# Both scans of a chunk pair back to back on VectorE, its statistics and normalise behind them

## The reference, cut to what matters

```
z = sigmoid(h @ Wz.T + bz);  t = tanh(h @ Wh.T + bh)      # here Wz = Wh, bz = bh
a = clip(1 - z, 1e-8, 1 - 1e-8)
s[i] = a[i] * s[i-1] + z[i] * t[i]                        # along the sequence
h = layernorm(s + h if layer > 0 else s) * gamma + beta
```

## Time and profile before

| | |
|---|---|
| median of 3 runs | 461.15 us (461.13 to 468.23) |
| the profiled execution, its own time | 462.03 us |
| its span, first to last instruction | 460.2 us |
| mean granted TensorE clock | 0.917 |
| busy share of the span: PE, DVE, ACT, POOL | 78%, 70%, 49%, 39% |

### The profile page before, as it was taken

How to read it: one execution, slowest core, us unless ns; L and a number is a source line. 1 busy time by engine, 2 the same in 40 slices (tenths; PEclk the granted TensorE clock), 3 DMA queues, 4 the chain that set the end, 5 groups by cost and what they waited for, 6 DMA issues and landing times.

```text
span 460.2 us, 8251 instructions
## 1 busy us (share of the span) xinstructions
PE 359.6 (78%) x2861; PEld 278.6 (61%) x2861; DVE 323.2 (70%) x917; ACT 227.5 (49%) x402; POOL 179.5 (39%) x278
## 2 busy tenths in 40 slices
PE   1666767676674459886799799999699989997991
PEld 1245636354362246655678668968568868785791
DVE  6988987988977665868527927688928687447416
ACT  2435786988955254336225257434267424623520
POOL 6235563656546306720038400259400268403211
PEclk9997898999977588889599989999989999999998
DMA  5600000000000000000000000000000000000000
GB/s 159 191 0 0 3 1 0 1 0 2 1 0 0 1 1 1 1 0 1 1 1 2 2 1 2 1 0 23 0 0 0 0 0 25 1 3 0 24 0 24
DMA packets 8968, 5.48 MB, mean 12 GB/s; under 512 B 700, under 2 KB 8424, under 8 KB 8936
## 3 DMA queue, kind: packets, MB, share of 16 engines
q1 hardware_dynamic: 8936, 5.07, 3.8%
HBM read 4.02 MB, written 1.05 MB: 11 GB/s over the span
## 4 chain that ended last, share of the span: by engine, by line
PE 52%; DVE 24%; ACT 12%; issue 9%; POOL 1%; DMA 1%; POOLq 0%; DVEq 0%; ACTq 0%
PE bank L761 9%; PE bank L694 5%; PE bank L658 5%; PE bank L502 4%; ACT work L921 3%; PE bank L528 3%; PE bank L746 3%; PE bank L669 2%; PE bank L671 2%; PE bank L540 2%; PE bank L747 2%; PE bank L751 2%; PE bank L542 2%; DVE tmp L285 2%; DVE tmp L288 2%
## 5 line engine op out<-in xcount | busy, mean ns | idle before, releaser
L469 POOL TENSOR_TENSOR h_fwd<-ident_bf,mneg 128x512 bf16<-128x512 bf16 x32 | 33.1, 1041 | 81.8 <-DVE mneg L1251 59.7
L1004 ACT ACTIVATE z_and_t<-bank,vec 128x512 f32<-128x512 f32 x64 | 43.8, 694 | 41.8 <-PE bank L751 41.7
L761 PE MATMUL bank<-w_s,z_and_t 128*128 128x128 f32 x512 | 61.4, 277 | 0.0
L761 PEld LDWEIGHTS bank<-w_s,z_and_t 128*128 128x128 f32 x512 | 59.2, 192 | 3.1 <-ACT z_and_t L1004 2.3
L988 ACT ACTIVATE probs<-bank 128x512 f32<-128x512 f32 x64 | 37.7, 595 | 42.9 <-PE bank L671 42.9
L1255 DVE TENSOR_REDUCE mx<-bank 128x4 f32<-128x512 f32 x64 | 43.6, 686 | 21.2 <-PE bank L658 20.4
L446 POOL TENSOR_TENSOR a_bwd<-a_bwd,a_fwd 128x512 f32<-128x512 f32 x11 | 14.6, 1327 | 102.7 <-DVE a_fwd L1312 102.7
L658 PE MATMUL bank<-k_st,q_m 128*128 128x128 f32 x256 | 48.0, 313 | 8.2 <-DVE mx L1255 7.1
L658 PEld LDWEIGHTS bank<-k_st,q_m 128*128 128x128 f32 x256 | 40.3, 205 | 11.2 <-DVE mx L1255 5.4
L540 PE MATMUL bank<-ident,work 128*128 128x128 f32 x128 | 37.4, 319 | 10.7 <-DVE work L1136 7.9
L502 PE MATMUL bank<-ident,work 128*128 128x128 f32 x144 | 25.5, 306 | 10.8 <-DVE work L296 6.8
(11 more groups left out here) (179 smaller groups left out, 866.8 us busy)
## 6 DMA issues: line engine op xcount, KB each, us to landing
x_rows<-in_x_dram SPq DMA_DIRECT2D x4, 256.0 KB, 3.1
probs<-in_L_ffn_W_dram SPq DMA_DIRECT2D x1, 1024.0 KB, 5.4
w_s<-in_L_ffn_W_dram SPq DMA_DIRECT2D x4, 256.0 KB, 6.3
out_dram<-ctx_rows SPq DMA_DIRECT2D x3, 256.0 KB, 2.2
ctx_rows<-in_ctx_dram SPq DMA_DIRECT2D x1, 256.0 KB, 3.2
out_dram<-ctx_rows SPq DMA_DIRECT2D x2, 128.0 KB, 1.8
fw_rows<-in_L_xcond_fusion_W_dram SPq DMA_DIRECT2D x1, 128.0 KB, 3.9
wq_s<-in_L_ffn_Wq_dram SPq DMA_DIRECT2D x1, 64.0 KB, 3.0
```

The costliest lines, as they stand in the source:

```text
L469: pool.tensor_tensor(diag_of(j), ident_bf[:, :].unsqueeze(1).to_broadcast([P, 4, P]), mneg[:, t % 2, 4 * j:4 * j + 4].unsqueeze(2).to_broa ...
L761: last = pe.matmul(dst[:, t * P:(t + 1) * P], hid[:, e % 2, c, t * P:(t + 1) * P], w2_s[:, e, c, :], start=(c == 0), stop=(c == FC - 1))
L1004: act.activation(hid[:, e % 2, c, :], bank[6 + (c + flip) % 2][:, :], ACT.Relu, bias=col(R_B1 + FC * e + c)).then_inc(s["relu_r"], 1)
```

## The change

Only VectorE's window is reordered. The same instructions run with the same waits; nothing is added or removed. Before, the order is: inflow(2j), stats(2j-2), scan(2j), stats(2j-1), inflow(2j+1), norm(2j-4), scan(2j+1). After it is: inflow(2j), scan(2j), inflow(2j+1), scan(2j+1), stats(2j-2), stats(2j-1), norm(2j-4). It holds for all pairs of all four layers; the two windows behind the last pair (scans=False) keep their order.

```diff
                 if scans:
                     inflow(l, 2 * j, layer0)
                     link()
-                if rows:
-                    stats(l, 2 * j - 2)
                 if scans:
                     scan(l, 2 * j, layer0)
                     link()
-                if rows:
-                    stats(l, 2 * j - 1)
                 if scans and not layer0:
                     inflow(l, 2 * j + 1)
-                before_norm()
-                if normed:
-                    norm(l, 2 * j - 4)
                 if scans:
                     link()
                     scan(l, 2 * j + 1, layer0)
                     link()
+                if rows:
+                    stats(l, 2 * j - 2)
+                    stats(l, 2 * j - 1)
+                before_norm()
+                if normed:
+                    norm(l, 2 * j - 4)
```

## The result

The kernel after takes 499.81 us (median of 4 runs, 498.04 to 502.38) against 461.14 us before: 1.082 times as long, interval 1.077 to 1.087. Its profiled execution took 498.04 us, with a span of 496.2 us (36.0 more than before) and a mean granted clock of 0.885.

What follows compares the result with a forecast made beforehand. It took a loop of waits between TensorE and ScalarE to bound the kernel, and the change to close a loop through VectorE's norm: 5.0 us in layer 0 plus 27.0 over 12 windows of 9.7 us gave 493 us, range 481 to 502.

Steps and rivals of the forecast that it cites:

- clock always low: Case that TensorE's clock is low at the norm in every window: 497 to 501 us, chance 0.18.
- Layer 0: Layer 0: later stats delay layer_norm and decay, so its last norm ends at 50.3 instead of 45.37, 5.0 us.
- The loop through norm: Norm, to_rows, affine, gates, second inflow, scan, stats, norm: 8.90 us per window, 10.22 at the low clock.
- The loop through GpSimd: Stats, layer_norm, next decay, first scan, second inflow: inflow could start at E + 4.1, against E + 4.18 over TensorE.
- The clock: TensorE's transposes take 1.32 us more at the low level, expected in six windows of ten: 9.7 us per window.
- the second rival: Clock low at each norm, the same period repeating the same state: 10.22 us per window, 499 us, chance 0.18.
- One wait removed alone would give nothing back: The ways over GpSimd and TensorE come to the same length, so removing either wait alone gains nothing.
- What follows the windows: Behind the last norm with scans: rows unchanged, about 325 us as before, 2 us either way for the clock.
- only the hole: Rival: norm's place does not matter, only VectorE's unfilled 1.6 us per window: 12.8 us more, 474 us, chance 0.05.
- faster: Rival: the second scan ends sooner and releases the odd to_rows sooner: 447 to 452 us, chance 0.02.
- covered: Rival: VectorE's 0.71 us slack and the time before gate_in absorb it: within 2%, up to 470 us, chance 0.04.
- The clock is low at each norm: Rival: TensorE's pause right ahead of the transposes lowers the clock every window: 38.2 us more, 499 us, chance 0.18.

Runs made afterwards that it cites:

- e3_gates_first: Kernel after, with ScalarE doing gates(2j+1) ahead of affine(2j-6): 489.75 us, ratio 1.060 against the kernel before.
- e4_decay_first: Kernel after, with GpSimd doing the next window's first decay ahead of layer_norm in layers 1 to 3: 494.60 us, ratio 1.071 against the kernel before.
- e10_both_pauses: Kernel after, with five unread TensorE matmuls per window of layers 1 to 3, two ahead of the second gate_in, three behind: 490.15 us, ratio 1.058.
- b_act_only: Kernel before, with ScalarE's gates(2j+1) ahead of affine(2j-6) as the one edit: 452.69 us, ratio 0.977.
- e1_norm_mid: Kernel after, with VectorE's norm back ahead of the second scan and both stats still last: 501.75 us, ratio 1.086 against the kernel before.

## Why the prediction was right, and where it was off

The prediction was 493 us with 481 to 502; 499.8 was measured. The two loops and the part of the clock came out as described. The size was 6.8 us short, and by the list of chances the time falls into the class "clock always low" (497 to 501, 0.18) and not into that of the forecast (487 to 497, 0.45), although the clock behaved as the forecast had it.

- **Layer 0.** 5.0 us were predicted, and the norm at its end at 50.3. It ended at 50.30, 4.9 us late, and the first scans of pairs 2 and 3 started at 36.20 and 45.13, where 36.2 and 45.1 were predicted.
- **The loop through norm.** 10.22 us were predicted at the low clock. The window from 67.70, in which the clock was low over the whole way through TensorE, took 10.29: 0.14 + 2.84 + 2.52 + 4.79, against 0.15 + 2.83 + 2.52 + 4.72. TensorE's L540 waited for L1136 in every window. Shown by e3_gates_first, in which the loop is cut and no window is longer than 9.18.
- **The loop through GpSimd.** I had it at about 8.8 us and below the other one's 8.90 at the high clock. It is the longer one there: 9.16 us, against 9.0 for the loop through norm (e4_decay_first). The stretch from the stats' end to the first scan is 4.31 us (I left 0.08 between decay and scan out), and two steps inside VectorE were too short: from first scan to second inflow it is 1.33 us where I took 1.12, and from inflow to scan 0.73 where I took 0.60. Both prices came from rows of before in which another operation, that did not have to wait for the first one's result, stood second. (The two stats in a row take 0.07 less than I added up.) For the same reason VectorE's sum of one window does not stay at 6.46 us, as the prediction has it: from start to start it is 6.77.
- **The clock.** I took six windows in ten at the low level and a period of 9.7 us. It was 9.79: four of the twelve windows took 9.16, the others 9.59 to 10.29. Measured by the loops as they are (9.16 and 10.29), 0.63 us of 1.13 is a share of 0.56. The share was right, and the forecast period came out 0.1 too short by the term above. Only its direction was argued, from the idle share and the place of the second pause; that six in ten was so close is luck. TensorE's rows show something that I had missed. In the eight windows with the clock low behind the norm the longer of the two pauses just before was 2.00 to 2.31 us, in the four others 1.64 to 1.88 us. And a low window leaves the next one a shorter pause (1.00 us ahead of the gate_in at 76.75, after 2.31 ahead of that at 66.30). That fits the long and short windows taking turns, against the second rival's "a period that is the same each time repeats the same state". It is no rule for one pause alone: in before the clock stayed at 1.00 through five windows with pauses of 2.31 us. Of the signs, the granted clock of the stage came out at 0.85 (from 50 to 162 us), at the edge of the "below 0.85". e10_both_pauses shows what the low level costs: 7.2 us.
- **One wait removed alone would give nothing back.** Half right. At the low clock the loop through norm is the longer by 1.1 us, so e3_gates_first took 7.4 us off the windows (10 off the median). e4_decay_first, which cuts the loop over GpSimd, took 0.7 us off them, as said.
- **What follows the windows.** I allowed 2 us; it came to 3.0 us, so the sign "about 325 us as before" failed. Up to the first maximum of the scores (L1255, in after L1254) it takes 36.0 us in before and 38.0 in after, at a granted clock of 0.75 and 0.67 in these 35 us. In e4_decay_first, with the clock at 0.74, the rest is 325.0 us, in e3_gates_first at 0.66 it is 328.4. In b_act_only, with VectorE's order of before, it is 327.7 at 0.72. So the 3 us are not tied to the reordering itself. That fits a clock that falls or not by where the pauses happen to lie, but no run was made to test it, and the cause stays open.
- **The medians.** The profiled execution of after lies 1.8 us below its median, that of before 0.9 us above. So 36.0 us in the spans are 38.7 us in the medians. Of the 7 us between forecast and result, 1.0 lies up to the last norm with scans, 3.0 in the rest, and the other 2.7 between profiled executions and medians.

Of the rivals, "only the hole" is out by e3_gates_first and "faster" and "covered" by the result. "The clock is low at each norm" came nearest in time, 499 us, but not in what happened: four of the twelve windows took 9.16 us, with the clock at 1.00 over the norm and the transposes behind it. That it met the time is chance: it had 5.1 us more in the windows than were measured, and lacked the 5.7 us of the rest and of the medians.

The Trainium skill's rule for it (TensorE: Matmul & The Clock Gate, Part 1), half rate after idling and full rate after work, agrees with e10_both_pauses, in which TensorE idled for at most 1.04 us at a time and its granted clock stayed at 1.00 in eleven windows. In after the clock fell in eight windows of twelve; in the other four it stayed up through pauses of up to 1.88 us.

## What to carry to other kernels

Where several engines follow orders written by hand, price an exchange by who gets which input later: operations that feed other engines (here the stats) belong as early in the window as their inputs allow, unless they then push back one that feeds a longer loop, as the norm did in e1_norm_mid. Draw every loop of waits from one operation back to the same operation in the next window and add it up; here two loops of 9.16 us and of 9.0 to 10.3 us lay on top of each other, so that cutting one took 0.7 or 7.4 us off the windows and cutting both 27.8. And when one such loop is found, look for an operation that waits with a ready one behind it on the same engine: exchanging these two on ScalarE made the kernel before 2.3% faster (1.6 to 3.0%).

## What the runs showed of the hardware

- In these rows an operation of VectorE that waits for the result of the one before it starts later than another that does not. Inflow to a scan that reads its result: 0.73 us (83.71 to 84.44); inflow to stats: 0.61 us (92.67 to 93.28). Scan to an inflow that overwrites what it read: 1.33 us (82.38 to 83.71); scan to stats: 1.14 us (84.44 to 85.58). The differences are 0.12 and 0.19 us, and the loop over GpSimd holds each of the two once per window. The second operation is also of another kind each time, and no run separates that from the wait; but two kinds that do not wait, stats and norm, start 0.61 and 0.60 us behind an inflow. The Trainium skill, VectorE: DVE Perf Modes, section "The DRAIN you can't avoid", has it that the semaphore costs nothing extra, from a measurement of tensor_copy alone. The rows here point the other way for these operations.
- The granted clock can rise while TensorE does nothing but transposes: in after they are all that it does from 88.64 to 92.96 us, back to back, and the clock goes from 0.50 to 1.00 at about 92.2. Their spacing goes from 0.21 to 0.11 us.
- Adding 5 unread matmuls per window made the kernel 9.7 us faster than after by keeping the granted clock at 1.00, while adding only three of them left it within 1 us of after: a pause of 2.3 us was still there.
